# The lead-in of a metaformer kernel reordered: w1's turns between pair 0's spreads, pair 0's tile before pair 1's statistics, one w2 block moved to ScalarE

## The chip, the cores and the metric

One core of a Trainium2 chip runs the kernel. The metric is the device time of one execution in microseconds (us); the median of three runs is given. A core has a matrix engine (TensorE, in the rows PE, with its weight loads as PEld), a vector engine (VectorE, DVE), a scalar engine (ScalarE, ACT), GpSimd (POOL) and SyncE (SP), which issues most of the DMAs. Each runs its own list of instructions strictly in the order in which it is written, and waits on semaphores that the others raise. TensorE's clock has two levels, 1.2 and 2.4 GHz; the profile gives the granted level as a share of full.

## What is computed

```python
x = x + conv_ref(ln_c(x), fc1_w, fc2_w, sa_w)     # LayerNorm over channels, channel gate, 7x7 token gate
t = to_tokens(x)                                  # 16 images of 24x8 -> 3072 tokens of 512 channels
t = t + ffn_ref(ln_t(t), w1, w2)                  # bitlinear(512->2048), gelu, bitlinear(2048->512)
# bitlinear: w_quant = clip(round(w * rms), -1, 1) / rms, with rms = rsqrt(mean(w*w));
#            x_quant = clip(round(x * 127/max|x|)) / scale, one scale for each token
```

The attention part needs for each image the mean and maximum of each channel over the tokens (through two small matrices, the channel gate), and for each token the mean and maximum over the channels (through a 7x7 convolution, the token gate). The two feed-forward weights must be squared and summed before they can be rounded to -1, 0, 1.

## The kernel before, in words

Sixteen images are worked in 8 **pairs** of two images; a pair is 384 tokens, that is three **tiles** of 128 tokens (tile 0.2 is pair 0, tile 2). Nothing reorders: the order on each engine is the order of the calls in the source. Ahead of the loop over the pairs stands a lead-in of some 70 us in which pair 0's attention, both weights' preparation, pair 1's attention and the first tiles' feed-forward are woven by hand. The loop body for pair c then does tile c.2 and the next pair's tiles 0 and 1 of the first matmul (`ffn_in`), all of the second (`ffn_out`), and the attention of pair c+2.

The functions that the change touches, by engine:

- **TensorE**: `turn_x` turns a tile of the input into PSUM; `spread_ca` spreads the channel gate over a tile's tokens; `turn_weights(k, raw, banks)` turns blocks of w1 (k = 0) or w2 (k = 1) into two PSUM banks `ps_t`, a block being 8 transposes, and waits until the block two earlier has been copied out; `conv` is the 42 small matmuls of the token gate; `turn_v1(pair, k, bank)` turns channel block k of the normalised pair into the PSUM bank `front`, three transposes; `turn_xq` turns a rounded tile; `ffn_in(tile, banks, blocks)` is four blocks of four 128x512 matmuls; `weight_mean(k)` sums the squares over the partitions.
- **ScalarE**: `copy_x`, `copy_xq` and `copy_weights` copy these out of PSUM; `token_mean(pair, k)` takes the channel means of a `front` bank, and only then may the next `turn_v1` into that bank start; `squares` sums a weight's squares; `gelu`; `centre`; `gate_tokens`; `sum_channels`; `pack_g` packs the rounded hidden tile for the DMA that turns it. The first gelu brings an ACT_TABLE_LOAD.
- **VectorE**: `token_max` (channel maxima of a `front` bank), `scale_channels`, `split_stats` (two subtractions that `conv` waits for), `sum_conv`, `token_gate`, `add_attention`, `row_stats`, `limit` (a tile's scale), `channel_stats`/`aggregate` (the LayerNorm statistics of a pair; `stats1` is both), `round_weights(1, ...)` (w2's rounding), `hidden_max`/`hidden_scale`, and the blocks of `copy_weights` that `BY_VECTOR` gives it: a clip out of PSUM and a second step in SBUF.
- **GpSimd**: `normalise1` (a pair's LayerNorm), `round_weights(0, ...)` (w1's rounding, 8 pieces), `rstd2`, `round_x`, `round_g`.

A block of w1 or w2 is written w1[n], w2[n] below, n from 0 to 7. In the lead-in pair 0's spreads are followed by pair 1's three `turn_x`, then w1[0], w1[1], `conv(pair0)`, and w1[2] to w1[7]. The first matmuls of the feed-forward, `ffn_in(0.0)` blocks 0 to 3, alternate with pair 1's four `turn_v1`; `weight_mean(1)` (the start of w2's rounding) stands between the third of these and block 1. The lead-in ends with `conv(pair1)` and w2[7], and the loop starts with `ffn_in(0.2)`.

Of the kernel before, what the change touches and what calls it, by code (L numbers as in the profile page):

```python
# [5 lines left out]
def metaformer_kernel(nc, x, fc1_w, fc2_w, sa_w, w1, w2, out):  # L6
# [22 lines left out]
    NT = TOK // P  # L29
# [15 lines left out]
    with ctx:  # L45
# [234 lines left out]
        BY_VECTOR = [(1, 3), (1, 5)]  # L280
# [133 lines left out]
        def _(pool):  # L414
# [112 lines left out]
            normalise1(Pair(1), 0, 1, 2)  # L527
            rstd2(Tile(Pair(0), 0))
            round_x(Tile(Pair(0), 0))
            rstd2(Tile(Pair(0), 1))  # L530
# [38 lines left out]
        def _(act):  # L569
# [123 lines left out]
            gate_channels(pair0)  # L693
            squares(1, w2_raw, w2_loaded, (0,))
            copy_caT(pair0)
            for s in range(NT):
                sum_channels(Tile(pair0, s))
            for s in range(NT):
                copy_x(Tile(pair1, s), (s + 1) % 2)
            act.wait_ge(masks_ready, 2)  # L700
            copy_weights(0, (0, 2))
            gate_tokens(pair0)
            copy_weights(0, (4, 5, 6))
            centre(Tile(pair0, 0))
            copy_weights(0, (7,))
            squares(1, w2_raw, w2_loaded, (1,))
            copy_xq(Tile(pair0, 0), 0)
            token_mean(pair1, 0, 1)
            squares(1, w2_raw, w2_loaded, (2,))
            gelu(Tile(pair0, 0), None, h_start, (0,))  # L710
            centre(Tile(pair0, 1))
# [23 lines left out]
            copy_weights(1, (6,))  # L735
# [79 lines left out]
        def _(dve):  # L815
# [265 lines left out]
            row_stats(Tile(pair0, 0))  # L1081
            limit(Tile(pair0, 0))
            token_max(pair1, 0, 1)
            squares(1, w2_raw, w2_loaded)
            add_attention(Tile(pair0, 1))
            row_stats(Tile(pair0, 1))
            weight_sum(1)
# [25 lines left out]
            copy_weights(1, (5,))  # L1113
            split_stats(pair1)
            hidden_max(Tile(pair0, 1), 0)
            stats1(pair2, 0, 1, 2)
            hidden_max(Tile(pair0, 1), 1)
# [80 lines left out]
        def _(pe):  # L1198
# [203 lines left out]
            b = spread_ca(Tile(pair0, 1), 1, b)  # L1402
            a = spread_ca(Tile(pair0, 2), 0, a)
            b = turn_x(Tile(pair1, 0), 1, b)
            a = turn_x(Tile(pair1, 1), 0, a)
            b = turn_x(Tile(pair1, 2), 1, b)
            turn_weights(0, w1_raw, (0, 1))
            pe.wait_ge(band_ready, 2)
            conv(pair0)
            turn_weights(0, w1_raw, (2, 3, 4, 5, 6, 7))  # L1410
            weights_ready(0)
            b = turn_v1(pair1, 0, 1, b)
            a = turn_xq(Tile(pair0, 0), 0, a)
            ffn_in(Tile(pair0, 0), h_start, (0,))
            b = turn_v1(pair1, 1, 1, b)
# [26 lines left out]
            b = turn_x(Tile(pair2, 2), 1, b)  # L1442
            conv(pair1)
            turn_weights(1, w2_raw, (7,))

            def body(pair, attend, normalise, turn):
# [9 lines left out]
                ffn_in(Tile(pair, 2))  # L1456
# [98 lines left out]
```

## Time and profile before

| | us |
|---|---|
| median of 3 runs | 291.81 (291.41 to 291.82) |
| the profiled execution, its own time | 290.93 |
| its span, first to last instruction | 289.2 |
| PE busy | 256.5 (89% of the span) |
| DVE busy | 230.0 (80%) |
| ACT busy | 229.0 (79%) |
| POOL busy | 159.8 (55%) |
| lead-in, until the loop's first matmul | 71.1 |

The profile's rows give start, duration and instruction, groups of like ones merged as x8; in square brackets stands how long the engine was idle before, and on whose work it waited. A group of matmuls ends some 0.2 us after the next may start, since they are pipelined. The page's 40 slices show TensorE between 10 and 90% busy up to about 80 us, and at 90% or more in every later slice but the last; its granted clock is below full in two stretches of the lead-in.

### The profile page before, as it was taken

What the parts mean: (1) busy time and instruction counts of PE and PEld (TensorE: products, weight loads), DVE (VectorE), ACT (ScalarE), POOL (GpSimd) and SP (SyncE); (2) the same over time, 40 slices, a digit from 0 to 9 for tenths busy, and PEclk for the clock granted to TensorE, in tenths of its full rate; (3) what the DMA queues carried; (4) which work ended last, traced back from release to release, by engine and by line L of the source; (5) the groups of instructions that cost most, each with busy time, mean ns of one, the idle gap of its engine ahead of it and who ended that gap; (6) DMA issues with size and microseconds to landing.
All of it is one profiled execution on the core that took longest, in us unless ns stands there. A gap on an engine that the chain in (4) does not pass through costs nothing.

```text
span 289.2 us, 5900 instructions
## 1 busy us (share of the span) xinstructions
PE 256.5 (89%) x1842; PEld 153.2 (53%) x1850; DVE 230.0 (80%) x535; ACT 229.0 (79%) x467; POOL 159.8 (55%) x265
## 2 busy tenths in 40 slices
PE   1655948976899999999999999999999999999995
PEld 1434734644446565656565656565656555544544
DVE  0573778999888898889888988898889887998531
ACT  0775779895887889788978897889798977898541
POOL 8414863233774487448744874487448743376330
PEclk9999975998999999999999999999999999999999
DMA  7999700000334235633562356235603550373757
GB/s 190 389 384 423 228 24 2 1 0 2 73 76 106 77 75 123 140 105 75 125 166 75 73 129 157 82 74 128 131 3 72 130 126 20 57 181 73 124 98 215
DMA packets 71622, 34.20 MB, mean 118 GB/s; under 512 B 52584, under 2 KB 68968, under 8 KB 71080
## 3 DMA queue, kind: packets, MB, share of 16 engines
q1 hardware_dynamic: 69844, 32.78, 44.4%
q10 hardware_dynamic: 1748, 1.05, 1.3%
q8 instruction: 15, 0.25, 0.3%
q14 instruction: 15, 0.12, 0.1%
HBM read 14.94 MB, written 6.29 MB: 73 GB/s over the span
## 4 chain that ended last, share of the span: by engine, by line
PE 68%; DVE 9%; ACT 8%; issue 6%; POOL 2%; DMA 2%; ACTq 2%; another core or an unknown queue 1%; POOLq 0%; DVEq 0%; SPq 0%
PE ps_o L1299 22%; PE ps_h L1286 12%; PE ps_t L1286 12%; PE front L1214 4%; PE front L1204 3%; PE front L1329 3%; PE small L1260 3%; PE small L1230 2%; DMA hq<-w_raw 2%; PE front L1269 2%; PE small L1224 1%; ACT junk_p L578 1%; ACTq L345 1%; DVE amax L946 1%; ACT junk L578 1%
## 5 line engine op out<-in xcount | busy, mean ns | idle before, releaser
L1299 PE MATMUL ps_o<-w2T,hq 128*128 128x512 f16 x352 | 85.2, 379 | 0.8 <-DMA hq<-w_raw 0.8
L515 POOL TENSOR_SCALAR w_room<-w_room,q 128x1024 f32<-128x1024 f32 x48 | 53.6, 1127 | 23.7 <-DVE q L956 23.0
L946 DVE TENSOR_REDUCE amax<-w_room 128x1 f32<-128x1024 f32 (+1 forms) x48 | 57.9, 1206 | 6.5 <-ACT w_room L578 6.5
L1286 PE MATMUL ps_h<-w1T,xq 128*128 128x512 f16 x208 | 53.1, 393 | 0.7 <-ACT xq L578 0.7
L578 ACT ACTIVATE w_raw<-w_room 128x1024 f16<-128x1024 f16 x46 | 48.4, 1055 | 4.3 <-POOL w_room L515 3.5
L1299 PEld LDWEIGHTS ps_o<-w2T,hq 128*128 128x128 f16 x352 | 33.5, 98 | 32.4 <-DMA hq<-w_raw 1.3
L1286 PE MATMUL ps_t<-w1T,xq 128*128 128x512 f16 x176 | 42.6, 379 | 0.0
L578 ACT ACTIVATE w_room<-ps_h,s 128x512 f32<-128x512 f32 x52 | 35.5, 685 | 6.6 <-PE ps_h L1286 5.8
L578 ACT ACTIVATE w_room<-ps_t,s 128x512 f32<-128x512 f32 x44 | 29.6, 690 | 6.4 <-PE ps_t L1286 6.2
L1286 PEld LDWEIGHTS ps_h<-w1T,xq 128*128 128x128 f16 x208 | 19.9, 102 | 20.1 <-issue 2.7
L504 POOL TENSOR_SCALAR cen<-cen,q 128x512 f32<-128x512 f32 x24 | 16.7, 695 | 21.2 <-DVE q L938 21.2
L1286 PEld LDWEIGHTS ps_t<-w1T,xq 128*128 128x128 f16 x176 | 17.2, 98 | 20.8
L578 ACT ACTIVATE junk_m<-front 128x192 bf16<-128x192 f32 x64 | 20.5, 328 | 6.7 <-DVE pooled L857 6.6
L1204 PE MATMUL front<-id,x_in 128*128 128x128 f32 x96 | 17.1, 313 | 7.9 <-DMA x_in<-in_x 6.1
L844 DVE BATCH_NORM_STATS2 st<-xt 128x6 f32<-128x512 f32 x24 | 15.5, 679 | 8.3 <-ACT xt L578 8.3
L1214 PE MATMUL front<-id,v 128*128 128x128 f32 x96 | 17.7, 306 | 4.6 <-ACT w1T L578 1.6
L918 DVE SCALAR_TENSOR_TENSOR t<-pv,sg,xt 128x512 f32<-128x512 f32 x24 | 21.5, 894 | 0.3
L479 POOL TENSOR_SCALAR ve<-mv 128x1 f32<-128x1 f32 x24 | 5.1, 211 | 29.5 <-DVE mv L926 28.9
L886 DVE CUSTOM_DVE_ANT_0 pv<-v,front 128x512 f32<-128x512 f32 x24 | 15.8, 685 | 5.7 <-remote 4.6
L578 ACT ACTIVATE cen<-t,mv 128x512 f32<-128x512 f32 x24 | 17.3, 721 | 3.8 <-DVE mv L926 3.8
L857 DVE TENSOR_REDUCE pooled<-front 128x2 f32<-128x384 f32 x32 | 17.6, 551 | 3.1 <-PE front L1214 2.8
L492 POOL TENSOR_SCALAR v<-xt,minus_mean,rs 128x512 f32<-128x512 f32 x24 | 19.0, 800 | 1.4
(136 smaller groups left out, 470.1 us busy)
## 6 DMA issues: line engine op xcount, KB each, us to landing
out<-w_room SPq DMA_DIRECT2D x15, 384.0 KB, 3.4
x_in<-in_x SPq DMA_DIRECT2D x14, 384.0 KB, 4.1
w_room<-in_L_ffn_w SPq DMA_DIRECT2D x4, 1024.0 KB, 8.8
w_raw<-in_L_ffn_w SPq DMA_DIRECT2D x4, 1024.0 KB, 11.7
x_in<-in_x ACTq DMA_DIRECT2D x2, 384.0 KB, 3.9
hq<-w_raw SPq DMA_TRANSPOSE x48, 3.1
out<-w_room SPq DMA_DIRECT2D x3, 128.0 KB, 1.9
fc_raw<-in_L_conv_fc_w ACTq DMA_DIRECT2D x2, 128.0 KB, 4.4
```

The costliest lines, as they stand in the source:

```text
L492: pool.tensor_scalar(v1[:, s, :], xt[pair.par][:, s, :], minus_mean[:, s:s + 1], rs1[:, s:s + 1], ALU.add, ALU.mult).then_inc(normed, 1)
L504: pool.tensor_scalar(c[:, :], c[:, :], q1[tile.par][:, 0:1], MAGIC, ALU.mult, ALU.add).then_inc(cen_rounded, 1)
L515: pool.tensor_scalar(part, part, q2[tile.par][:, 0:1], MAGIC, ALU.mult, ALU.add).then_inc(g_rounded, 1)
L578: act.activation(out_ap, in_ap, func, **more).then_inc(signal, 1)
L857: dve.tensor_reduce(pooled[:, k, 0:2], front[bank][:, 0:TOK].rearrange("p (i t) -> p i t", i=2), AX.X, ALU.max).then_inc(max_ready, 1)
L886: dve.tensor_tensor_reduce(out=pv[tile.pair.par][:, tile.s, :], in0=v1[:, tile.s, :], in1=front[bank][:, :], scale=1.0, scalar=-3.0e38, op ...
L918: chain.mark(dve.scalar_tensor_tensor(t_tile, pv[par][:, s, :], sg[par][:, s:s + 1], xt[par][:, s, :], ALU.mult, ALU.add))
L946: chain.mark(dve.tensor_reduce(amax2[:, i:i + 1], w1_room[:, first + i * F // 2:first + (i + 1) * F // 2 + i], AX.X, ALU.max, apply_absolu ...
L1204: last = pe.transpose(front[bank][:, tile_cols(k)], x_in[tile.pair.par][:, k, tile_cols(tile.s)], id32[:, :])
L1214: last = pe.transpose(front[bank][:, tile_cols(s)], v1[:, s, tile_cols(k)], id32[:, :])
L1286: last = pe.matmul(banks[b], xq[tile.pair.par][:, tile.s, k, :], w1T[:, k, b * 512:(b + 1) * 512], start=(k == 0), stop=(k == NC - 1))
L1299: last = pe.matmul(out_bank(tile)[:, :], hq[tile.par][:, k, :], w2T[:, k, :], start=(k == 0), stop=(k == NF - 1))
```

## The change

Only the order of the lead-in is changed, and which engine copies w2[5].

- TensorE: w1[0] is turned between pair 0's second and third spread, w1[1] after pair 1's first `turn_x`, w1[2] after the second; the third `turn_x` goes behind `conv(pair0)`. `turn_xq(0.0)` and `ffn_in(0.0)` block 0 go ahead of pair 1's first `turn_v1`. At the end, w2[7] and blocks 0 and 1 of `ffn_in(0.2)` go ahead of `conv(pair1)`; the loop's first body then has only blocks 2 and 3 of that tile.
- ScalarE: `copy_caT` goes ahead of one `squares` of w2; w1[0] is copied ahead of pair 1's `copy_x`; `centre(0.0)` two blocks earlier against the copies; `token_mean(pair1, 0)` goes behind the second and third `squares` of w2 and gelu block 0; w2[5] is added.
- VectorE: w1[1] is copied ahead of `split_stats(pair0)`; pair 1's statistics are cut in two, the third tile and `aggregate` behind `row_stats(0.0)`; `add_attention` and `row_stats(0.1)` ahead of the `squares` of w2 and pair 1's first `token_max`; w2[5] is taken away; `split_stats(pair1)` goes behind `stats1(pair2)`.
- GpSimd: `normalise1(pair1)` goes behind `rstd2(0.0)` and `round_x(0.0)`.

```diff
-        BY_VECTOR = [(1, 3), (1, 5)]
+        BY_VECTOR = [(1, 3), (1,)]
 # gpsimd
-            normalise1(Pair(1), 0, 1, 2)
             rstd2(Tile(Pair(0), 0))
             round_x(Tile(Pair(0), 0))
+            normalise1(Pair(1), 0, 1, 2)
 # scalar
             gate_channels(pair0)
+            copy_caT(pair0)
             squares(1, w2_raw, w2_loaded, (0,))
-            copy_caT(pair0)
...
             copy_xq(Tile(pair0, 0), 0)
-            token_mean(pair1, 0, 1)
             squares(1, w2_raw, w2_loaded, (2,))
             gelu(Tile(pair0, 0), None, h_start, (0,))
+            token_mean(pair1, 0, 1)
             centre(Tile(pair0, 1))
...
-            copy_weights(1, (6,))
+            copy_weights(1, (5, 6))
 # vector
+            copy_weights(0, (1,))
             split_stats(pair0)
             weight_units(0)
-            copy_weights(0, (1,))
-            stats1(pair1, 0, 1, 2)
+            channel_stats(pair1, 0, 1)
             sum_conv(pair0)
...
-            copy_weights(1, (5,))
-            split_stats(pair1)
             hidden_max(Tile(pair0, 1), 0)
             stats1(pair2, 0, 1, 2)
+            split_stats(pair1)
 # tensor
             b = spread_ca(Tile(pair0, 1), 1, b)
+            turn_weights(0, w1_raw, (0,))
             a = spread_ca(Tile(pair0, 2), 0, a)
...
             weights_ready(0)
-            b = turn_v1(pair1, 0, 1, b)
             a = turn_xq(Tile(pair0, 0), 0, a)
             ffn_in(Tile(pair0, 0), h_start, (0,))
+            b = turn_v1(pair1, 0, 1, b)
             b = turn_v1(pair1, 1, 1, b)
...
+            turn_weights(1, w2_raw, (7,))
+            ffn_in(Tile(pair0, 2), blocks=(0, 1))
             conv(pair1)
-            turn_weights(1, w2_raw, (7,))
```

**Place 1**, TensorE from pair 0's spreads (`front<-caT,img_pick`) to the second of the feed-forward's first blocks (`ps_h<-w1T,xq`). `front<-id,x_in` is `turn_x`, `ps_t<-id,w_room` w1's turns, `small<-ch_stat` the convolution, `front<-id,v` `turn_v1`, `ps_o<-w_sum` `weight_mean`. Before:

```order
L1246 MATMUL front<-caT,img_pick 128x512 x3
L1204 MATMUL front<-id,x_in 128x128 x12
L1354 MATMUL ps_t<-id,w_room 128x128 x16
L1260 MATMUL small<-ch_stat,band 128x3 x18
...
L1354 MATMUL ps_t<-id,w_room 128x128 x48
L1214 MATMUL front<-id,v 128x128 x3
L1269 MATMUL front<-id,cen 128x128 x4
L1286 MATMUL ps_h<-w1T,xq 128x512 x4
L1214 MATMUL front<-id,v 128x128 x6
L1338 MATMUL ps_o<-w_sum,inv_n 128x1
L1286 MATMUL ps_h<-w1T,xq 128x512 x8
```

TensorE at the same place, in the changed kernel:

```order
L1249 MATMUL front<-caT,img_pick 128x512 x2
L1357 MATMUL ps_t<-id,w_room 128x128 x8
L1249 MATMUL front<-caT,img_pick 128x512
...
L1357 MATMUL ps_t<-id,w_room 128x128 x8
L1263 MATMUL small<-ch_stat,band 128x3 x18
...
L1357 MATMUL ps_t<-id,w_room 128x128 x40
L1272 MATMUL front<-id,cen 128x128 x4
L1289 MATMUL ps_h<-w1T,xq 128x512 x4
L1217 MATMUL front<-id,v 128x128 x9
L1341 MATMUL ps_o<-w_sum,inv_n 128x1
L1289 MATMUL ps_h<-w1T,xq 128x512 x8
```

Three of w1's blocks moved ahead of the convolution, and pair 1's first `turn_v1` moved behind block 0, so that three of them now stand in a row ahead of `weight_mean` and block 1.

**Place 2**, ScalarE from the last of w1's copies (`w1T<-ps_t`) to gelu block 1 (`w_room<-ps_h`). `junk,w_sq<-w_raw` is a `squares` of w2, `junk_m,pooled<-front` is `token_mean`, two instructions for one channel block. Before:

```order
L578 ACTIVATE w1T<-ps_t,sharp_bias 128x4x256
L578 ACTIVATE junk,w_sq<-w_raw 128x2048
L578 ACTIVATE xq<-front 128x512
L578 ACTIVATE junk_m,pooled<-front 128x192 x2
L578 ACTIVATE junk,w_sq<-w_raw 128x2048
L578 ACT_TABLE_LOAD
L578 ACTIVATE w_room<-ps_h,s_0 128x512
L578 ACTIVATE cen<-t,mv_1 128x512
L578 ACTIVATE w_room<-ps_h,s_0 128x512
```

ScalarE at the same place, in the changed kernel:

```order
L578 ACTIVATE w1T<-ps_t,sharp_bias 128x4x256 x2
L578 ACTIVATE junk,w_sq<-w_raw 128x2048
L578 ACTIVATE xq<-front 128x512
L578 ACTIVATE junk,w_sq<-w_raw 128x2048
L578 ACT_TABLE_LOAD
L578 ACTIVATE w_room<-ps_h,s_0 128x512
L578 ACTIVATE junk_m,pooled<-front 128x192 x2
L578 ACTIVATE cen<-t,mv_1 128x512
L578 ACTIVATE w_room<-ps_h,s_0 128x512
```

The channel means of pair 1's block 0 moved behind a `squares`, the table load and the first gelu.

**Place 3**, VectorE at the end of the lead-in: `amax<-w_room` is `hidden_max`, `w2T` the two steps of copying w2[5], `ch_stat<-ch_stat` `split_stats(pair1)`, `st<-xt` and `mv<-st` `stats1(pair2)`, `conv_sum` `sum_conv(pair1)`. Before:

```order
L956 RECIPROCAL q_0<-lim 128x1
L1023 TENSOR_SCALAR w2T<-ps_t 128x8x128
L1026 TENSOR_SCALAR w2T<-w2T 128x8x128
L899 TENSOR_TENSOR ch_stat<-ch_stat 128x6
L900 TENSOR_TENSOR ch_stat<-ch_stat 128x6
L946 TENSOR_REDUCE amax<-w_room 128x1
L844 BN_STATS st<-xt 128x6 x3
L850 BN_AGGR mv<-st 128x2 x3
L946 TENSOR_REDUCE amax<-w_room 128x1
...
L905 TENSOR_REDUCE conv_sum<-small 128x3
```

VectorE at the same place, in the changed kernel:

```order
L958 RECIPROCAL q_0<-lim 128x1
L948 TENSOR_REDUCE amax<-w_room 128x1
L846 BN_STATS st<-xt 128x6 x3
L852 BN_AGGR mv<-st 128x2 x3
L901 TENSOR_TENSOR ch_stat<-ch_stat 128x6
L902 TENSOR_TENSOR ch_stat<-ch_stat 128x6
L948 TENSOR_REDUCE amax<-w_room 128x1
...
L907 TENSOR_REDUCE conv_sum<-small 128x3
```

The two steps of w2[5] are gone, and the subtractions that `conv(pair1)` waits for moved behind the statistics of pair 2.

## Rows read from the trace of the kernel before

**Rows 1.** Windows: length, busy PE, PEld, DVE, ACT, POOL; PEclk, DMA share, GB/s.

```profile
102.72:131.59 28.87, 28.76 (x209) 17.04 (x209) 25.65 (x62) 25.32 (x56) 18.01 (x31) 1.00 0.48 111
...
39.49:49.73 10.24, 6.85 (x32) 4.08 (x30) 7.44 (x16) 10.20 (x15) 4.68 (x10) 0.50 0.01 2
49.73:70.20 20.47, 15.38 (x168) 10.55 (x168) 19.48 (x43) 17.72 (x40) 7.56 (x10) 1.00 0.00 1
70.20:73.60 3.40, 3.40 (x23) 1.79 (x20) 3.33 (x9) 2.27 (x3) 1.03 (x2) 0.50 0.00 0
```

**Rows 2.** Timeline of PE: start, us, line, operation, [idle before <-releaser].

```profile
29.48 1.95 PE L1204 MATMUL front<-id,x_in 128*128 128x128 f32 x8
...
33.54 0.60 PE L1260 MATMUL small<-ch_stat,band 128*128 128x3 bf16 x18
...
45.50 1.89 PE L1286 MATMUL ps_h<-w1T,xq 128*128 128x512 f16 x4 [0.69 <-ACT xq L578]
47.18 1.49 PE L1214 MATMUL front<-id,v 128*128 128x128 f32 x6
...
49.00 2.23 PE L1286 MATMUL ps_h<-w1T,xq 128*128 128x512 f16 x8
...
62.05 0.63 PE L1204 MATMUL front<-id,x_in 128*128 128x128 f32 x4
...
69.19 0.61 PE L1260 MATMUL small<-ch_stat,band 128*128 128x3 bf16 x18 [2.01 <-DVE ch_stat L900]
...
71.08 3.15 PE L1286 MATMUL ps_h<-w1T,xq 128*128 128x512 f16 x8
...
82.24 1.89 PE L1286 MATMUL ps_h<-w1T,xq 128*128 128x512 f16 x8
```

**Rows 3.** Timeline of POOL: w1's rounding, and pair 1's normalising.

```profile
26.10 8.80 POOL L460 TENSOR_SCALAR w_room<-w_room,w_rms 128x1024 f32<-128x1024 f32 x8
...
38.83 2.60 POOL L492 TENSOR_SCALAR v<-xt,minus_mean,rs 128x512 f32<-128x512 f32 x3
```

**Rows 4.** Timeline of DVE.

```profile
31.65 1.06 DVE L900 TENSOR_TENSOR ch_stat<-ch_stat 128x6 f32<-128x6 f32 x1
...
50.00 1.29 DVE L1006 TENSOR_SCALAR w_raw<-w_raw,w_rms 128x2048 f32<-128x2048 f32 x1 [0.20 <-POOL w_rms L452]
...
70.18 1.86 DVE L844 BATCH_NORM_STATS2 st<-xt 128x6 f32<-128x512 f32 x3
...
72.31 1.19 DVE L946 TENSOR_REDUCE amax<-w_room 128x1 f32<-128x1025 f32 x1
...
73.87 0.17 DVE L905 TENSOR_REDUCE conv_sum<-small 128x3 f32<-128x9 f32 x1
...
74.74 1.24 DVE L918 SCALAR_TENSOR_TENSOR t<-pv,sg,xt 128x512 f32<-128x512 f32 x1
...
100.87 0.17 DVE L900 TENSOR_TENSOR ch_stat<-ch_stat 128x6 f32<-128x6 f32 x1
```

**Rows 5.** Timeline of ACT.

```profile
42.83 1.92 ACT L578 ACTIVATE junk<-w_raw 128x2048 bf16<-128x2048 f32 x1
...
44.85 0.60 ACT L578 ACTIVATE xq<-front 128x512 f16<-128x512 f16 x1
45.34 0.33 ACT L578 ACTIVATE junk_m<-front 128x192 bf16<-128x192 f32 x1
...
47.98 1.28 ACT L578 ACT_TABLE_LOAD   x1
...
50.47 0.69 ACT L578 ACTIVATE w_room<-ps_h,s 128x512 f32<-128x512 f32 x1
...
67.75 0.63 ACT L578 ACTIVATE xt<-front 128x512 f32<-128x512 f32 x1
71.33 1.11 ACT L578 ACTIVATE w2T<-ps_t,sharp_bias 128x1024 f16<-128x1024 f16 x1 [2.94 <-PE ps_t L1354]
72.34 1.99 ACT L578 ACTIVATE w_raw<-w_room 128x1024 f16<-128x1024 f16 x2
```

More of the change, by code:

```diff
@@ L693, in _ @@
             gate_channels(pair0)
+            copy_caT(pair0)
             squares(1, w2_raw, w2_loaded, (0,))
-            copy_caT(pair0)
             for s in range(NT):
                 sum_channels(Tile(pair0, s))
-            for s in range(NT):
-                copy_x(Tile(pair1, s), (s + 1) % 2)
             act.wait_ge(masks_ready, 2)
-            copy_weights(0, (0, 2))
+            copy_weights(0, (0,))
+            copy_x(Tile(pair1, 0), 1)
+            copy_x(Tile(pair1, 1), 0)
+            copy_weights(0, (2,))
             gate_tokens(pair0)
-            copy_weights(0, (4, 5, 6))
+            copy_x(Tile(pair1, 2), 1)
+            copy_weights(0, (4, 5))
             centre(Tile(pair0, 0))
-            copy_weights(0, (7,))
+            copy_weights(0, (6, 7))
             squares(1, w2_raw, w2_loaded, (1,))
             copy_xq(Tile(pair0, 0), 0)
-            token_mean(pair1, 0, 1)
             squares(1, w2_raw, w2_loaded, (2,))
             gelu(Tile(pair0, 0), None, h_start, (0,))
+            token_mean(pair1, 0, 1)
             centre(Tile(pair0, 1))
@@ L1081, in _ @@
             row_stats(Tile(pair0, 0))
+            channel_stats(pair1, 2)
+            aggregate(pair1, 0, 1, 2)
             limit(Tile(pair0, 0))
-            token_max(pair1, 0, 1)
-            squares(1, w2_raw, w2_loaded)
             add_attention(Tile(pair0, 1))
             row_stats(Tile(pair0, 1))
+            squares(1, w2_raw, w2_loaded)
+            token_max(pair1, 0, 1)
             weight_sum(1)
@@ L1402, in _ @@
             b = spread_ca(Tile(pair0, 1), 1, b)
+            turn_weights(0, w1_raw, (0,))
             a = spread_ca(Tile(pair0, 2), 0, a)
             b = turn_x(Tile(pair1, 0), 1, b)
+            turn_weights(0, w1_raw, (1,))
             a = turn_x(Tile(pair1, 1), 0, a)
-            b = turn_x(Tile(pair1, 2), 1, b)
-            turn_weights(0, w1_raw, (0, 1))
+            turn_weights(0, w1_raw, (2,))
             pe.wait_ge(band_ready, 2)
             conv(pair0)
-            turn_weights(0, w1_raw, (2, 3, 4, 5, 6, 7))
+            b = turn_x(Tile(pair1, 2), 1, b)
+            turn_weights(0, w1_raw, (3, 4, 5, 6, 7))
             weights_ready(0)
-            b = turn_v1(pair1, 0, 1, b)
             a = turn_xq(Tile(pair0, 0), 0, a)
             ffn_in(Tile(pair0, 0), h_start, (0,))
+            b = turn_v1(pair1, 0, 1, b)
             b = turn_v1(pair1, 1, 1, b)
@@ L1454, in body @@
                     a = a + b
-                ffn_in(Tile(pair, 2))
+                ffn_in(Tile(pair, 2), blocks=range(FB) if pair.c > 0 else (2, 3))
                 if pair.c > 0:
```

## The prediction, made before the changed kernel had run

> **What bounds the kernel now.** I read the windows first. From 102.7 to 131.6 us, one pair of the loop, TensorE is busy 28.76 of 28.87 us [rows 1], and the pairs after it look alike: the loop runs at the pace of TensorE's own instructions. The change leaves the loop alone but for two blocks that its first body no longer has, so whatever the lead-in gains or loses until pair 1's first feed-forward block (82.24 us [rows 2]) is handed on unchanged to the end. That instant is my end mark. No single engine bounds the lead-in: from 39.5 to 49.7 ScalarE is busy 10.20 of 10.24 us, from 49.7 to 70.2 VectorE 19.48 of 20.47 [rows 1]. There an instruction that is late makes all behind it late, and an engine that waits can't make that up.
>
> The clock belongs to the picture. It is at half (1.2 GHz) from 39.5 to 49.7 and from 70.2 to 73.6 us [rows 1]. Up to 32.7 us the page prints full, but eight turns of x take 1.95 us there against 0.63 for four later [rows 2], so that stretch is cold too. It rose at 49.7 after TensorE had worked since 45.50 without a gap to speak of, and fell at 70.2 after a wait of 2.01 us ahead of the convolution [rows 2].
>
> **w1's turns, first part (27 to 43 us).** Block 1 of w1 is now turned by about 31.4 us: the first turn of x starts near 29.48, four turns take half of 1.95, and a block's eight narrower turns about as long (an estimate from that row). VectorE clips it until 32.1. Its second step and both subtractions of `split_stats` then lie inside GpSimd's rounding of w1, which runs without a gap, 1.10 us a piece, until 34.9 [rows 3]. What that does is in the trace: the second subtraction started at 31.65, took 1.06 us and ended at 32.71, as the sixth piece did (26.10 + 6 x 1.10 = 32.70); in the loop the same instruction takes 0.17 [rows 3, 4]. So I let the three steps end with a piece each, at 32.7, 33.8 and 34.9, and the convolution start at 35.0 instead of 33.54. Bounds: 33.9 if one step slips between two pieces, 33.0 if none waits.
>
> The Trainium skill ("SBUF — State Buffer", section "Who interferes with whom") says that a VectorE instruction with two SBUF inputs and a GpSimd instruction that reads SBUF exclude each other for the whole instruction. By that the three steps wait as I have it; a plain 0.17 each would put the convolution at 33.0 and the sum below some 0.8 us lower. The 1.06 us row agrees with the rule.
>
> Behind the convolution VectorE has two of pair 1's three statistics (0.62 each [rows 4]) instead of three, so tile 0's gate, scale and rounding gain what the late convolution loses. ScalarE has the same instructions as before up to the last copy of w1, with one long wait instead of several short ones. I take nothing for this part: the `squares` that followed that copy at 42.83 [rows 5] still starts there. Bounds: 1.1 us earlier (one piece less waited for) to 0.8 later (w1's later turns at half clock). Tile 0's rounding may be ready earlier, but `copy_xq` stands behind that `squares`, so it stays at 44.85 [rows 5] and block 0 at 45.50 [rows 2].
>
> **Pair 1's channel means, second part (45 to 54 us).** This is the term that decides. Before, `token_mean` of channel block 0 ran at 45.34, ahead of the other `squares` [rows 5], and freed its bank for the second `turn_v1` at 47.18 [rows 2]. Now ScalarE does: `squares` 45.34 to 47.36 (2.02, as 42.83 to 44.85), table load 1.28 to 48.65, gelu block 0 0.6 (0.69 less the overlap), and the two means 0.6 (45.34 to the next `squares`, which ends 2.03 later at 47.98): 49.9 [rows 5]. The first turn itself waits for GpSimd's normalising (2.60 [rows 3] plus small steps, behind tile 0's rounding), which ends near 47.5, with block 0 (45.50 + 1.89): no extra cost, and TensorE idles from about 48.3 to 49.9. Behind that second turn stand, on TensorE, the third, `weight_mean(1)` and block 1. Before, 1.82 us passed from 47.18 to block 1 at 49.00 [rows 2], at half clock; at full clock half of it. So block 1 starts between 50.8 and 51.7, 1.8 to 2.7 late. Blocks 1 and 2 took 2.23 with the clock rising inside [rows 2]; all at full they take 1.89, as the eight at 82.24, all at half 3.15, as the eight at 71.08. Gelu block 1 (50.47 [rows 5]) and w2's first rounding (50.00 [rows 4]) are late by 1.5 us if the clock is up from 49.9, by up to 3.6 if it stays down. TensorE's busy stretch now has a hole of 1.6 us where it had none, so I expect the rise later than at 49.7: I take 2.5, the middle. VectorE carries it on, since it has no slack until 70.
>
> **The end of the lead-in, third part.** w2[5] leaves VectorE and costs ScalarE 1.01 (71.33 to 72.34 [rows 5]). The last `copy_x` of pair 2 ended at 68.38 (67.75 + 0.63): now 69.4 + S, with S the 2.5. Behind it VectorE does the third statistic 0.62, the aggregate 0.27 (72.04 to 72.31), two subtractions 0.34 (GpSimd's pieces are over by then), then `hidden_max` to `sum_conv` 1.56 (72.31 to 73.87) [rows 4]: 72.2 + S against 73.87, S minus 1.7. This is where w2[5] and the 2.01 us wait at 69.19 [rows 2] are paid back. The convolution must be over by then: with blocks 0 and 1 ahead of it at full clock (1.73) it is, about 71.8 + S; at half (3.15) it ends near 73.2 + S, 1.0 late. For that I add 0.35, a third. ScalarE reaches `pack_g` at 67.75 + 1.0 + 0.5 + 1.0 + S = 70.25 + S against 72.34 [rows 5], +0.4, less than the other path: w2[7] turned early is hidden. `add_attention` at 74.74 took 1.24 [rows 4], part of it a wait for GpSimd's normalising of pair 2; between 0 and 0.5 of that may go, I take 0.25.
>
> **Sum.** 0 + 2.5 - 1.7 + 0.35 - 0.25 = +0.9 us at the end mark and so at the end: 290.93 becomes 291.8 in the profiled execution's time (span 289.2, 1.7 around it), and the median of 291.81 becomes 292.7. A measurement of this kernel tells about 0.2%, 0.6 us, from no change.
>
> **Rivals.**
> 1. *Faster.* The denser stretch of turns from 27 us on raises the clock before block 1 is turned, near 30.5. Then the clip ends within GpSimd's piece before, the convolution starts at 33.9, and all of the second part starts 1.1 earlier: S = 1.4 to 1.5, the end at full clock, and -1.7 + 1.45 - 0.5 gives -0.8: 291.0. For it: w1's turns fill waits of TensorE there. Against: the clock rose only at 32.7 in spite of the turns since 29.48.
> 2. *No difference.* The clock returns at 49.7 as before, S is 1.5, and the payback of 1.7 covers it: -0.2 plus 0 to 0.5, 291.6 to 292.1. For it: the rise needn't depend on the hole of 1.6 us.
> 3. *Worse.* The clock falls again while TensorE waits for the late convolution at 33 to 35, w1's turns 3 to 7 go at half clock (+0.8), or S is over 3: +1.5 to +2.2, 293.3 to 294.0.
> 4. *It does not do what it says:* pair 0's tile is no earlier, because `copy_xq` keeps its place behind the `squares`. That is in my sum already.
>
> **How the numbers follow.** Forecast (+0.6 to +1.4) 0.39; rival 1 0.21; rival 2 0.25; rival 3 0.15. Some of rival 2 and a little of the forecast's lower end make "same" 0.26; slower 0.53; faster 0.21. The range goes down to rival 1's 290.9 and up to 293.8 in rival 3; what it leaves out, faster than that or over +2.0, is about 2 in 10.
>
> **What would show it.** In the changed kernel's trace: the convolution of pair 0 near 35.0; the last w1 copy's follower on ScalarE near 42.8; TensorE waiting over 1 us for `junk_m` ahead of the second turn of v, near 49.9; w2's first rounding at 51.5 to 52.7; `sum_conv` of pair 1 near 75; the first block of pair 1 near 83.1. If the second turn of v starts before 48.5, or VectorE's first w2 rounding before 51, the term that decides is wrong and the change is even or faster; if the loop's period is not 28.9, the handing on is.

## The result, and the profile after

The changed kernel takes 294.22 us in the median (293.9 to 296.85, 6 runs) against 291.67 (291.27 to 292.12) for the kernel before on the same chip: a ratio of 1.0101, 95% interval [1.0065, 1.0137]. The ratio weighs all executions, the one of 296.85 among them; the quotient of the medians is 1.0087. By the medians that is 2.55 us slower, where +0.9 was forecast and the range ended at +2.0. The profiled execution took 294.05 us, its span is 292.3, against 290.93 and 289.2.

The windows first (length, busy PE, PEld, DVE, ACT, POOL; PEclk, DMA share, GB/s). The first stretch is one in which TensorE's clock is at half from end to end, the second is one pair of the loop:

```profile
43.84:57.49 13.65, 8.81 (x30) 4.55 (x31) 5.92 (x13) 8.38 (x22) 6.96 (x11) 0.50 0.00 0
105.73:134.60 28.87, 28.76 (x209) 17.03 (x209) 25.64 (x62) 25.32 (x56) 18.00 (x31) 1.00 0.52 111
```

The loop is what it was, 28.87 us for a pair [rows 1], so the lead-in made all the difference. In it the half clock lasts 13.65 us and no engine is busy for even two thirds of the time: everybody waits. Before, the half clock lasted 10.24 us with ScalarE busy throughout [rows 1].

TensorE's timeline (start, us, line, operation, [idle before <-releaser]):

```profile
34.26 0.60 PE L1263 MATMUL small<-ch_stat,band 128*128 128x3 bf16 x18 [1.18 <-DVE ch_stat L902]
...
35.80 1.06 PE L1357 MATMUL ps_t<-id,w_room 128*128 128x128 f16 x16
...
43.08 0.38 PE L1272 MATMUL front<-id,cen 128*128 128x128 f16 x4 [2.82 <-POOL cen L504]
44.60 1.89 PE L1289 MATMUL ps_h<-w1T,xq 128*128 128x512 f16 x4 [1.15 <-ACT xq L578]
49.00 0.90 PE L1217 MATMUL front<-id,v 128*128 128x128 f32 x3 [2.51 <-POOL v L492]
51.47 1.51 PE L1217 MATMUL front<-id,v 128*128 128x128 f32 x6 [1.56 <-ACT junk_m L578]
...
53.06 3.57 PE L1289 MATMUL ps_h<-w1T,xq 128*128 128x512 f16 x8
...
74.00 1.90 PE L1289 MATMUL ps_h<-w1T,xq 128*128 128x512 f16 x8 [0.80 <-ACT xq L578]
...
85.25 1.89 PE L1289 MATMUL ps_h<-w1T,xq 128*128 128x512 f16 x8
```

Against [rows 2]: block 0 starts at 44.60 instead of 45.50, 0.90 us earlier. Then the first turn of v comes at 49.00 behind a wait of 2.51 for GpSimd, the next two at 51.47 instead of 47.18, and blocks 1 and 2 at 53.06 instead of 49.00, taking 3.57 instead of 2.23. Pair 1's first block comes at 85.25 instead of 82.24: +3.01, and the span is longer by 3.1.

The wait of 2.51 leads to GpSimd, and to what VectorE did meanwhile:

```profile
41.70 1.12 POOL L504 TENSOR_SCALAR cen<-cen,q 128x512 f32<-128x512 f32 x1 [1.38 <-DVE q L940]
42.80 0.26 POOL L508 TENSOR_SCALAR s<-lim,w_unit 128x1 f32<-128x1 f32 x1
43.14 2.29 POOL L485 TENSOR_SCALAR ve<-mv 128x3 f32<-128x3 f32 x1
45.52 0.87 POOL L486 TENSOR_TENSOR rs<-ve,half_pow 128x3 f32<-128x3 f32 x1
...
46.67 2.27 POOL L492 TENSOR_SCALAR v<-xt,minus_mean,rs 128x512 f32<-128x512 f32 x3
...
75.60 0.23 POOL L485 TENSOR_SCALAR ve<-mv 128x3 f32<-128x3 f32 x1 [1.36 <-DVE mv L852]
```

```profile
31.58 0.43 DVE L1028 TENSOR_SCALAR w1T<-w1T 128x1024 f16<-128x1024 f16 x1
31.92 1.09 DVE L901 TENSOR_TENSOR ch_stat<-ch_stat 128x6 f32<-128x6 f32 x1
33.05 1.06 DVE L902 TENSOR_TENSOR ch_stat<-ch_stat 128x6 f32<-128x6 f32 x1
...
43.12 2.26 DVE L991 CUSTOM_DVE_ANT_0 junk_v<-w_raw 128x2048 bf16<-128x2048 f32 x1
...
54.05 1.28 DVE L1008 TENSOR_SCALAR w_raw<-w_raw,w_rms 128x2048 f32<-128x2048 f32 x1 [0.19 <-POOL w_rms L452]
...
75.42 0.14 DVE L901 TENSOR_TENSOR ch_stat<-ch_stat 128x6 f32<-128x6 f32 x1
75.59 0.17 DVE L902 TENSOR_TENSOR ch_stat<-ch_stat 128x6 f32<-128x6 f32 x1
...
77.26 0.17 DVE L907 TENSOR_REDUCE conv_sum<-small 128x3 f32<-128x9 f32 x1
```

The first step of the normalising of pair 1, three numbers a partition, took 2.29 us at 43.14; the same step for pair 2 took 0.23 at 75.60. It began 0.02 us after VectorE's `squares` of w2, which multiplies a quarter of w2 with itself (two inputs, both in SBUF), and ended with it (43.12 + 2.26 = 45.38, against 45.43). The reverse is at 31.92 and 33.05, where VectorE's two subtractions of 0.14 and 0.17 (75.42, 75.59) took 1.09 and 1.06 beside GpSimd's rounding of w1. In the kernel before, the same `squares` ran from 44.43 to 46.71, within this idle time of GpSimd:

```profile
48.54 0.19 POOL L479 TENSOR_SCALAR ve<-mv 128x1 f32<-128x1 f32 x1 [4.15 <-DVE mv L926]
```

ScalarE, with the places that [rows 5] show of before:

```profile
42.07 1.91 ACT L578 ACTIVATE junk<-w_raw 128x2048 bf16<-128x2048 f32 x1
...
47.87 0.69 ACT L578 ACTIVATE w_room<-ps_h,s 128x512 f32<-128x512 f32 x1
50.59 0.33 ACT L578 ACTIVATE junk_m<-front 128x192 bf16<-128x192 f32 x1 [2.03 <-DVE pooled L859]
...
55.02 0.69 ACT L578 ACTIVATE w_room<-ps_h,s 128x512 f32<-128x512 f32 x1 [3.09 <-PE ps_h L1289]
```

Gelu of block 0 was done by 48.6, but `token_mean` waited for the first turn of v and VectorE's `token_max` behind it until 50.59, and gelu of block 1 came at 55.02 instead of 50.47: 4.55 late.

### The profile page after: what moved, and what is told of

Read it like the earlier page. It is cut to its first block, busy times and chain, and to the rows that moved or that the text cites. A ratio compares the mean times of both kernels' runs of the same rounds, so it can differ in the third digit from the quotient of the medians.

```text
span 292.3 us, 5899 instructions
## 1 busy us (share of the span) xinstructions
PE 255.2 (87%) x1842; PEld 152.4 (52%) x1850; DVE 227.9 (78%) x533; ACT 230.2 (79%) x468; POOL 161.1 (55%) x265
## 4 chain that ended last, share of the span: by engine, by line
PE 69%; DVE 11%; issue 7%; ACT 5%; POOL 2%; ACTq 2%; DMA 1%; POOLq 0%; DVEq 0%; SPq 0%
PE ps_o L1302 21%; PE ps_h L1289 13%; PE ps_t L1289 12%; PE front L1217 4%; PE front L1207 3%; PE front L1332 3%; PE small L1263 3%; PE small L1233 2%; PE front L1272 2%; DVE amax L948 2%; PE front L1249 2%; PE small L1227 1%; ACTq L345 1%; ACT junk_p L578 1%; DMA hq<-w_raw 1%
## 5 line engine op out<-in xcount | busy, mean ns | idle before, releaser
L1289 PE MATMUL ps_h<-w1T,xq 128*128 128x512 f16 x208 | 53.1, 393 | 1.9 <-ACT xq L578 1.9
L1207 PE MATMUL front<-id,x_in 128*128 128x128 f32 x96 | 16.3, 300 | 7.5 <-DMA x_in<-in_x 5.8
```

Source lines behind the costliest of these rows:

```text
L1207: last = pe.transpose(front[bank][:, tile_cols(k)], x_in[tile.pair.par][:, k, tile_cols(tile.s)], id32[:, :])
L1289: last = pe.matmul(banks[b], xq[tile.pair.par][:, tile.s, k, :], w1T[:, k, b * 512:(b + 1) * 512], start=(k == 0), stop=(k == NC - 1))
```

## The experiments

The three parts are named as in the prediction: w1's turns with the copies and statistics that go with them (one), pair 1's normalising, means and turns behind tile 0 (two), the end of the lead-in (three). Ratios are to the kernel before, run beside each; a difference of two ratios is put in us as its share of 291.7.

**The two suspects in the second part, one at a time.** First VectorE's `squares` out of the way of the normalising:

```diff
-            squares(1, w2_raw, w2_loaded)
             token_max(pair1, 0, 1)
+            squares(1, w2_raw, w2_loaded)
             weight_sum(1)
```

> The changed kernel with one move: VectorE's squares of w2's last quarter behind the first token_max of pair 1 instead of ahead of it, so that they no longer run while GpSimd starts pair 1's normalising. Theory: in the changed kernel that 2.26 us instruction held GpSimd's first 128x3 step from 43.14 to 45.43, and with it the three tiles of v and the first turn of v (49.00). Then the step takes 0.2 again, v is ready near 46.9, the first turn of v starts near 46.9, blocks 1 and 2 of tile 0 near 51.2 instead of 53.06, gelu of block 1 near 53.1 instead of 55.02, and the time is about 292.3 (294.2 less 1.9). Rival: the hold cost nothing, because the second turn of v waits for ScalarE's token_mean behind the table load and gelu of block 0 anyway: gelu of block 1 stays within 0.4 of 55.0 and the time at 293.8 to 294.4.

Measured: 292.86 us, ratio 1.0047 [1.0024, 1.0069]. Its GpSimd and TensorE:

```profile
43.90 0.19 POOL L485 TENSOR_SCALAR ve<-mv 128x3 f32<-128x3 f32 x1
...
45.33 2.26 POOL L492 TENSOR_SCALAR v<-xt,minus_mean,rs 128x512 f32<-128x512 f32 x3
```

```profile
36.11 1.91 PE L1357 MATMUL ps_t<-id,w_room 128*128 128x128 f16 x16
...
45.36 1.89 PE L1289 MATMUL ps_h<-w1T,xq 128*128 128x512 f16 x4 [1.15 <-ACT xq L578]
47.65 0.90 PE L1217 MATMUL front<-id,v 128*128 128x128 f32 x3 [0.40 <-POOL v L492]
50.08 1.51 PE L1217 MATMUL front<-id,v 128*128 128x128 f32 x6 [1.52 <-ACT junk_m L578]
```

Gelu of block 1 there:

```profile
54.02 0.69 ACT L578 ACTIVATE w_room<-ps_h,s 128x512 f32<-128x512 f32 x1 [3.48 <-PE ps_h L1289]
```

The step takes 0.19, the whole normalising 3.69 (43.90 to 47.59) instead of 5.80 (43.14 to 48.94), and the turns of v follow block 0 by 2.29 and 4.72 us, where in the changed kernel they followed by 4.40 and 6.87. The hold was there and cost some 2.1 us at the turns, 1.6 us in the time (1.0101 less 1.0047; 1.1 by the medians). The rival falls, though the theory's own instants were some 0.9 us too early (gelu of block 1 near 53.1): this execution's block 0 came 0.76 later than the changed kernel's.

Then the clock. `fill` issues matmuls whose output nobody reads:

```diff
+            def fill(n):
+                for i in range(n):
+                    pe.matmul(ps_h[1][:, :], img_pick[:, tile_cols(0)], caT[:, :], start=True, stop=True)
             turn_weights(0, w1_raw, (3, 4, 5, 6, 7))
+            fill(10)
             weights_ready(0)
             a = turn_xq(Tile(pair0, 0), 0, a)
+            fill(4)
             ffn_in(Tile(pair0, 0), h_start, (0,))
+            fill(12)
             b = turn_v1(pair1, 0, 1, b)
+            fill(7)
             b = turn_v1(pair1, 1, 1, b)
```

> The changed kernel with TensorE's waits filled: 33 extra matmuls of 128x512 whose output nobody reads (10 behind w1's last turn, 4 behind the turn of tile 0, 12 behind block 0, 7 behind the first turn of v). Each takes about 0.22 us at full clock, so all of them fit in the waits if the clock holds. Theory: the clock fell at 43.84 and stayed half to 57.49 because TensorE waited; filled, it stays full, the turns of v and blocks 1 and 2 take 0.45, 0.75 and 1.8 us instead of 0.90, 1.51 and 3.57, gelu of block 1 comes near 53.2 instead of 55.02, and the time is about 292.4. The first turn of v stays at 49.0, since GpSimd's hold is untouched. Rival: the clock there doesn't hang on these waits (or blocks at half clock are covered by something else that is late): gelu of block 1 at 54.6 or later and 293.8 to 295.5, slower if the extra matmuls run at half clock and hold up the turns.

Measured: 292.57 us, ratio 1.0055 [1.0027, 1.0082]. The window in which the changed kernel's clock was at half, and blocks 1 and 2:

```profile
43.84:57.49 13.65, 11.80 (x69) 5.77 (x68) 7.70 (x15) 9.90 (x27) 8.05 (x11) 1.00 0.01 2
```

```profile
52.62 1.89 PE L1289 MATMUL ps_h<-w1T,xq 128*128 128x512 f16 x8
...
72.56 3.54 PE L1289 MATMUL ps_h<-w1T,xq 128*128 128x512 f16 x8 [0.79 <-ACT xq L578]
```

```profile
53.74 0.69 ACT L578 ACTIVATE w_room<-ps_h,s 128x512 f32<-128x512 f32 x1 [1.48 <-PE ps_h L1289]
```

With its waits filled TensorE has the full clock all through that window, blocks 1 and 2 take 1.89 instead of 3.57, and gelu of block 1 comes at 53.74 instead of 55.02. GpSimd's step still takes 2.29 here. The traced execution is itself one of the longer ones, 294.30 against the median of 292.57: it lost the gain again at 72.56, where two blocks ran at half clock ahead of the convolution, and pair 1's first block came at 85.59. So the trace shows the stretch, and the price of the half clock, about 1.3 us, rests on the timed runs (1.0101 less 1.0055).

Both edits at once (6 and 8 extra matmuls behind block 0 and the first turn, which come sooner):

> The changed kernel with both former edits at once: VectorE's squares of w2 behind the first token_max of pair 1, and TensorE's waits filled with 28 extra matmuls (10 behind w1's last turn, 4 behind the turn of tile 0, 6 behind block 0, 8 behind the first turn of v). Theory: the hold and the half clock are the two causes and add up: the first step of the normalising takes 0.2, the second turn of v still waits for token_mean and starts near 50.0, blocks 1 and 2 take 1.9, gelu of block 1 comes near 52.2 instead of 54.0 and 53.7 with one edit each, and the time is about 290.8 to 291.4, ratio 0.998 to 1.000: no slower than before. Rival: the two hide one another, since the wait for token_mean is what is left in both: 292.3 to 292.9, ratio 1.003 to 1.005.

Measured: 291.35 us, ratio 0.9988 [0.9968, 1.0009]. The two add up within the noise: 1.0101 to 0.9988 is 3.3 us, against 1.6 + 1.3. Taken from the changed kernel, each edit alone is only just clear of the intervals (0.54 and 0.46%, with some 0.42 and 0.45 either way, an estimate that adds the two intervals in squares); taken from one edit to both it is clearer, 0.67 and 0.59%, with some 0.34 and 0.30. What ends last ahead of block 1 is now neither, but the `squares` again, on VectorE's own list ahead of `weight_sum`:

```profile
51.25 0.38 PE L1341 MATMUL ps_o<-w_sum,inv_n 128*128 128x1 f32 x2 [0.44 <-DVE w_sum L997]
51.49 1.89 PE L1289 MATMUL ps_h<-w1T,xq 128*128 128x512 f16 x8
```

```profile
52.61 0.69 ACT L578 ACTIVATE w_room<-ps_h,s 128x512 f32<-128x512 f32 x1 [2.18 <-PE ps_h L1289]
```

The extra matmuls also fill waits that the kernel before has, where its clock is at half too [rows 1], so this kernel has a help that the kernel before lacks. Two later runs put extra matmuls at those places into kernels that are not late, and neither tells a gain from none (0.9926 for 0.9939, 0.9913 for 0.9900).

**The parts alone and in pairs.** The second part alone, on the kernel before (its lines in the diff ahead of the prediction, with pair 1's statistics left together where they were):

> The kernel before with the change's second part alone: pair 1's normalising behind tile 0's rounding, the first turn of v behind block 0, token_mean of channel block 0 behind the last squares and the first gelu, and VectorE's squares and token_max behind the second add_attention. Theory: block 0 stays at 45.5 (tile 0's rounding waits for ScalarE's centring at 41.2, not for GpSimd), the squares again hold the normalising for about 2 us and the turns of v and blocks 1 and 2 run at half clock, so gelu of block 1 is late by 5 us against the kernel before: 296 to 297, ratio 1.016 to 1.020. Rival: the second part frees GpSimd for tile 0's rounding and gives back the 0.9 us by which the changed kernel's block 0 came earlier, so that the first part is worth nothing: 295.0 to 295.6, ratio 1.012 to 1.014.

Measured: 297.52 us, ratio 1.0200 [1.0153, 1.0247]. On its GpSimd:

```profile
44.16 1.12 POOL L504 TENSOR_SCALAR cen<-cen,q 128x512 f32<-128x512 f32 x1 [2.31 <-DVE q L938]
45.26 0.26 POOL L508 TENSOR_SCALAR s<-lim,w_unit 128x1 f32<-128x1 f32 x1
45.60 2.29 POOL L485 TENSOR_SCALAR ve<-mv 128x3 f32<-128x3 f32 x1
```

The same hold of 2.29, and tile 0's rounding at 1.12 instead of the 0.69 that it takes undisturbed, beside the second `add_attention` that the part moved up. The ratio is at the theory's upper end, and one point of it was wrong: block 0 did not stay at 45.5, it came at 46.80. Not all of that is the part's doing: the profile of part three alone, which has the order of before up to there, has block 0 at 46.27.

The third part alone:

```diff
-        BY_VECTOR = [(1, 3), (1, 5)]
+        BY_VECTOR = [(1, 3), (1,)]
-            copy_weights(1, (5,))
-            split_stats(pair1)
             hidden_max(Tile(pair0, 1), 0)
             stats1(pair2, 0, 1, 2)
+            split_stats(pair1)
+            turn_weights(1, w2_raw, (7,))
+            ffn_in(Tile(pair0, 2), blocks=(0, 1))
             conv(pair1)
-            turn_weights(1, w2_raw, (7,))
```

> The kernel before with the change's third part alone: ScalarE copies w2's block 5, split_stats of pair 1 stands behind pair 2's statistics, w2's block 7 is turned and blocks 0 and 1 of tile 2 are computed ahead of the convolution of pair 1. Theory: the prediction's payback of 1.7 holds by itself: sum_conv of pair 1 near 72.2 instead of 73.87, the clock stays full at 70 since the wait of 2.01 us ahead of the convolution is filled, first block of pair 1 near 80.5 to 80.9 instead of 82.24, time 290.1 to 290.4. Rival: the payback was only late work catching up; TensorE's convolution is held by the two blocks ahead of it and the time stays at 291.3 to 291.9.

Measured: 289.64 us, ratio 0.9939 [0.9916, 0.9962]. The payback holds by itself in the timed runs. The profiled execution took 291.46, more than the median, and can't be set beside the profile before instant by instant (its block 0 is 0.77 later). It shows what the prediction had priced at a third of 1.0: the two blocks at half clock ahead of the convolution, and VectorE waiting for it.

```profile
69.72 3.55 PE L1285 MATMUL ps_h<-w1T,xq 128*128 128x512 f16 x8 [0.80 <-ACT xq L578]
```

```profile
74.36 0.17 DVE L905 TENSOR_REDUCE conv_sum<-small 128x3 f32<-128x9 f32 x1 [1.30 <-PE small L1259]
```

The same with 21 extra matmuls (8, 2 and 3 around tile 0's turn, 8 more into `ps_o` around the last turns of x and w2):

> The kernel before with the third part alone, and TensorE's waits filled with 21 extra matmuls of 128x512 (8 behind w1's last turn, 2 behind the first turn of v, 3 behind the turn of tile 0, and 2, 2 and 4 around the last turns of x and w2 at 66 to 70 us). Theory: with the clock full, block 0 of tile 0 and the turns of v behind it end some 1.5 us earlier, and blocks 0 and 1 of tile 2 take 1.9 us in every execution instead of 3.5 in some; VectorE and ScalarE bound the stretch from 50 us, so less than that arrives: 288.4 to 289.2, ratio 0.989 to 0.993, against 0.994 for the third part alone. Rival: those stretches are hidden behind VectorE and ScalarE, and the third part alone is as good: 289.5 to 289.9, ratio 0.993 to 0.995.

Measured: 290.06 us, ratio 0.9926 [0.9897, 0.9955]. The blocks ahead of the convolution take 1.90 at full clock there, and pair 1's first block comes at 81.39 against 82.75; but the two kernels' ratios cannot be told apart, so the filling isn't shown to be worth anything in the median.

Parts one and two, and parts two and three:

> The changed kernel with its third part put back (w2's block 5 on VectorE again, split_stats ahead of pair 2's statistics, the convolution of pair 1 ahead of w2's block 7 and of blocks 0 and 1 of tile 2). Theory: the parts nearly add up; the third is worth 1.8 us by itself (289.6 against 291.4), so without it the changed kernel comes to 295.7 to 296.3, ratio to the kernel before 1.015 to 1.017. Rival: the payback exists only where VectorE isn't late, and behind the late second part it was worth little: 294.3 to 295.0, ratio 1.010 to 1.012.

> The kernel before with the second and third parts. Theory: the parts add up, so this is the second part alone (ratio 1.020) less the third's 0.6 %: ratio 1.012 to 1.015, 294.9 to 296.1, above the changed kernel (1.010) by what the first part is worth there. Rival: the first part is worth nothing beside the second, and the ratio is the changed kernel's, 1.008 to 1.011.

Measured: 296.74 us, 1.0170 [1.0137, 1.0203], and 295.58 us, 1.0145 [1.0115, 1.0175]. Both are at the upper end of the theory's ratios, as sums of their parts. Adding the third part takes 0.55% (1.0200 to 1.0145) or 0.69% (1.0170 to 1.0101) off, adding the first 0.3% or 0.44%; single differences of this size are about as large as the intervals. TensorE in the profile of parts two and three:

```profile
32.75 1.91 PE L1353 MATMUL ps_t<-id,w_room 128*128 128x128 f16 x16
...
46.78 1.89 PE L1285 MATMUL ps_h<-w1T,xq 128*128 128x512 f16 x4 [0.69 <-ACT xq L578]
```

Parts one and three, with the second put back:

> The changed kernel with its second part put back: pair 1's normalising ahead of tile 0's rounding on GpSimd, the first turn of v ahead of tile 0's turn on TensorE, token_mean of channel block 0 ahead of the last squares on ScalarE, and on VectorE pair 1's last statistic behind w1's third block, token_max and then squares ahead of the second add_attention, as before. Parts one and three stay. Theory: part one is worth 0.9 us (block 0 at 44.6 instead of 45.5) and nothing of the second part's 5 us is left, part three pays 1.5 to 1.7: gelu of block 1 near 49.6 and the time 289.0 to 289.8, faster than both. Rival: part one's gain only exists because pair 1's normalising is out of the way; then block 0 is at 45.5 again and only part three is left, 290.0 to 290.4. Second rival: part three's payback is only a compensation for a late VectorE and is worth nothing when VectorE isn't late: 290.8 to 291.8.

Measured: 290.78 us, ratio 0.9977 [0.9954, 1.0]. This theory fell: the time is no better than part three alone (0.9939), rather worse. It lies at the second rival's edge, but that one is out, since part three is worth its 0.6% by itself. GpSimd and TensorE of that run:

```profile
39.50 0.20 POOL L485 TENSOR_SCALAR ve<-mv 128x3 f32<-128x3 f32 x1 [4.35 <-DVE mv L852]
...
43.61 0.19 POOL L479 TENSOR_SCALAR ve<-mv 128x1 f32<-128x1 f32 x1
...
45.30 0.69 POOL L504 TENSOR_SCALAR cen<-cen,q 128x512 f32<-128x512 f32 x1 [0.87 <-DVE q L940]
```

```profile
47.35 1.89 PE L1289 MATMUL ps_h<-w1T,xq 128*128 128x512 f16 x4 [0.69 <-ACT xq L578]
```

Pair 1's last statistic is now taken behind w1[3], so the normalising starts at 39.50; tile 0's small step stands behind it on GpSimd and starts at 43.61, and block 0 comes at 47.35, 1.85 later than in the profile before and 1.08 later than in that of part three alone. With the normalising ahead of tile 0, the late statistic costs more than the early turns give, in this trace and in the time (0.9977 for 0.9939). That suggested a repair, the statistics ahead of the convolution:

```diff
             turn_weights(0, w1_raw, (2,))
+            b = turn_x(Tile(pair1, 2), 1, b)
             conv(pair0)
-            b = turn_x(Tile(pair1, 2), 1, b)
 # scalar
+            copy_x(Tile(pair1, 2), 1)
             gate_tokens(pair0)
-            copy_x(Tile(pair1, 2), 1)
 # vector
-            channel_stats(pair1, 0, 1)
+            stats1(pair1, 0, 1, 2)
             sum_conv(pair0)
             copy_weights(0, (3,))
-            channel_stats(pair1, 2)
-            aggregate(pair1, 0, 1, 2)
```

> Parts one and three with the order of before in the second part, as once already, but pair 1's last tile is turned, copied and its statistics taken ahead of the convolution, so that pair 1's normalising no longer starts late (39.5 there, 37.4 in the kernel before). Theory: part one lost its 0.9 us in that run only because VectorE took pair 1's last statistic after w1's third block and GpSimd, in order, took tile 0's first small steps after the late normalising; with the statistics early the normalising starts near 36.5, tile 0's rounding near 42.5 instead of 43.46, block 0 near 44.6 to 45.0, and the time is 288.6 to 289.4, ratio 0.989 to 0.992, better than part three alone (0.994). Rival: w1's early turns give nothing that arrives, since ScalarE's copies and squares set tile 0's start: 289.6 to 290.2, ratio 0.993 to 0.996.

Measured: 288.81 us, ratio 0.9900 [0.9864, 0.9936]: faster than both kernels. Its GpSimd and TensorE:

```profile
36.55 0.20 POOL L485 TENSOR_SCALAR ve<-mv 128x3 f32<-128x3 f32 x1 [1.41 <-DVE mv L852]
...
42.36 0.69 POOL L504 TENSOR_SCALAR cen<-cen,q 128x512 f32<-128x512 f32 x1 [0.87 <-DVE q L940]
```

```profile
44.94 1.89 PE L1287 MATMUL ps_h<-w1T,xq 128*128 128x512 f16 x4 [1.03 <-ACT xq L578]
```

The normalising starts at 36.55, tile 0's rounding at 42.36, block 0 at 44.94, as the theory had them. With the 21 extra matmuls as well:

> The same kernel with the 21 extra matmuls of the earlier run with part three alone, in the same places (8, 2 and 3 around tile 0's turn, 2, 2 and 4 at 66 to 70 us). Theory: they keep the clock full in every execution, at 70 us above all, so the slow executions (0.5 % above the others) go: 288.0 to 289.0, ratio 0.987 to 0.990. Rival: where tile 0's rounding comes earlier the extra matmuls stand in its way (8 of them take 1.8 us at full and 3.5 at half clock): no better than without them, ratio 0.990 to 0.995.

Measured: 288.86 us, ratio 0.9913 [0.9880, 0.9945]: no better. The first eight took 3.28 us, partly at half clock, and block 0 came at 45.42. The rival fits the ratio; the two kernels cannot be told apart.

Part one alone, with that repair:

> The kernel before with the first part alone, pair 1's last tile and all its statistics ahead of the convolution (the order of the run with parts one and three). Theory: tile 0's rounding starts 1.1 us earlier than before (42.36 in that run's trace against 43.46), ScalarE's squares 0.4 to 0.7 earlier, and 0.3 to 1.0 us of it reach the end: ratio 0.9965 to 0.999. Rival: nothing reaches the end, because the turns of v and blocks 1 and 2 then run at half clock for longer (2.88 against 2.23 for the two blocks): ratio 0.999 to 1.001, no difference.

Measured: 290.31 us, ratio 0.9960 [0.9945, 0.9975]. The rival falls; the gain is at or a little past the theory's upper end.

## Why the prediction was wrong

Slower was right, the size was not. The sum had three terms, and the parts alone give each a measure (the ratio's share of 291.7 us):

| | forecast, us | alone | ratio alone |
|---|---|---|---|
| part one | 0 (-1.1 to +0.8) | -1.2, in the repaired order | 0.9960 |
| part two, S | +2.5 (1.5 to 3.6) | +5.8 | 1.0200 |
| part three | -1.7 + 0.35 - 0.25 = -1.6 | -1.8 | 0.9939 |
| all | +0.9 | +2.9 by the ratio, +2.55 by the medians | 1.0101 |

The total missed by less than S did, because part one's gain, which the sum took as nothing, offset a part of it. That the three ratios alone sum to +0.99%, so close to the change's 1.01%, is partly luck: part one stands there in the repaired order. As it was written it doesn't add up without part two, where it made things worse (0.9977 with part three, 0.9939 for part three alone).

**The step that failed is S, by the sentence "the first turn itself waits for GpSimd's normalising ..., which ends near 47.5 ...: no extra cost".** It ended at 48.94; unhindered, at the 3.69 of the first experiment, it would have ended at 46.8. The prediction had moved VectorE's `squares` and GpSimd's small steps, but had not asked what they would meet in their new places. Before, GpSimd stood idle while the `squares` ran. The rule was in hand: the first part's price rested on VectorE being held by GpSimd [rows 3, 4]. It was used in one direction only. By the Trainium skill ("SBUF — State Buffer", section "Who interferes with whom") a VectorE instruction with two SBUF inputs contends with a GpSimd instruction that reads SBUF, and of two that contend the one that issues first has the shared ports for the whole instruction while the other blocks. The trace agrees in both directions: 1.09 for 0.14, and 2.29 for 0.23.

**The clock was priced, but in the middle, and it stayed at half.** S was 1.5 with the clock up and 3.6 with it down, and 2.5 was taken. Counted from the start of block 0, gelu of block 1 came:

| | block 0 | gelu block 1 | between | more than before |
|---|---|---|---|---|
| before | 45.50 | 50.47 | 4.97 | |
| the changed kernel | 44.60 | 55.02 | 10.42 | 5.45 |
| `squares` out of the way | 45.36 | 54.02 | 8.66 | 3.69 |
| waits filled | 45.30 | 53.74 | 8.44 | 3.47 |
| both | 45.36 | 52.61 | 7.25 | 2.28 |

Without the hold, at half clock, the lateness is about the 3.6 of the forecast's bad end; the hold adds 1.8 (1.2 with the clock up) that no term had. With the hold gone and the clock up it is 2.28 instead of 1.5, of which 0.44 is a wait for the `squares` that the experiment moved. These are single executions; the timed runs say the same (1.0047, 1.0055, 0.9988): with either cause gone the time lies inside the forecast's range, with both gone it is the rival of no difference. With the hold there were two waits, 2.51 and 1.56, behind one of 2.82 ahead of tile 0's turn, and the half clock lasted to 57.49. The bad end itself was a little short: the 3.15 that it took for eight matmuls all at half [rows 2] runs past 73.60, the end of the stretch at half [rows 1]; all at half they take 3.57 here.

**Part one was the other miss, to the other side.** The three VectorE steps were not all blocked: the second step of w1[1], which has one input, took 0.43, the two subtractions waited, and the convolution came at 34.26. That is the case named for one step slipping between two of GpSimd's pieces (33.9), not the 35.0; the longest of the eight pieces took 1.40 there, the median one 1.12. `centre(0.0)`, which stands one copy earlier than before (not two, as the list of the change has it), started at 39.44 instead of 41.22, and ScalarE's `squares` at 42.07 instead of 42.83: the gain that had been taken as nothing with a bound of 1.1. Block 0 moves with the clock too. In the kernel before, w1[0] and w1[1] were turned at full clock:

```profile
32.62 1.09 PE L1354 MATMUL ps_t<-id,w_room 128*128 128x128 f16 x16
```

In the profile of parts two and three the same turns took 1.91, at half, and block 0 came at 46.78. With part one, the two blocks of w1 behind the convolution took 1.06 and block 0 came at 44.60 in the changed kernel's profile, 1.91 and 45.36 in the first experiment's. Like against like, block 0 comes 0.9 earlier than before where those turns ran at full clock, and 1.4 earlier with part one than without it where they ran at half. The timed runs with and without it put it at 0.3 to 0.4% (0.9 to 1.3 us).

**Part three came out.** sum_conv was put at S less 1.7: it is late by 3.39 (77.26 against 73.87), with S read at gelu block 3 of tile 0.1 as 5.04 (70.27 against 65.23), so less 1.65. The clock held at 74.00 (1.90 for the two blocks), so the 0.35 taken for it wasn't spent, and the end mark is at +3.01, another 0.38 less than sum_conv. The third that the prediction gave to the half clock there was fair: of the eight profiles of kernels with part three and no extra matmuls at that place, three show the two blocks at half (3.51 to 3.55) and five at full (1.90).

Of the signs named ahead, those of part one came early (the convolution at 34.26, ScalarE's `squares` at 42.07), and those of part two were right in kind and late: a wait of 1.56 for `junk_m` ahead of the second turn, at 51.47 instead of 49.9; w2's first rounding at 54.05 instead of 51.5 to 52.7; pair 1's first block at 85.25 instead of 83.1. The rival that pair 0's tile would come no earlier falls (44.60 for 45.50). The nearest rival was the third, worse, by its half clause that S is over 3. The handing on held: the loop's pair takes 28.87 as before.

What stays open: what part one as written would be worth alone, since the version of it that was timed alone takes pair 1's statistics elsewhere; and what decides from one execution to the next whether the clock is up at w1's turns and at the end of the lead-in, since each trace is one execution.

## What to carry to other kernels

When an instruction is moved, list what the other engine of the VectorE and GpSimd pair will be doing at the new place, in both directions: here a step of three numbers took 2 us longer because a VectorE instruction of 2.26 us with two SBUF inputs had started just before it. A wait that a reordering opens on TensorE can be paid twice, once as the wait and again in the matmuls behind it that run at half clock, as here, so price the two ends together and say which you expect, not the middle of one. Compare instants of two profiles only where the clock was at the same level up to there. And time the parts of a compound reorder separately: here two of three parts (one of them in a repaired order) were worth 1.0% together and the third lost 2.0%, which the sum hid.

## What the hardware showed that was not expected

GpSimd's 128x3 step was held for the whole of VectorE's 2.26 us `squares` in five traces (2.29 each time), and took 0.19 to 0.23 when it ran elsewhere. Extra matmuls that nobody reads kept TensorE at full clock for 13.65 us in which the changed kernel had half, which made blocks 1 and 2 take 1.89 instead of 3.57 us. The same order of instructions ran at either clock from one execution to the next: two blocks of w1 behind the convolution took 1.06 us in the changed kernel's profile and 1.91 in those of four kernels with the same order up to there.
